# Scans and statistics in two tasks each, one table set for exp and log, a new steady order, and written-out lists for the last two and a half batches

## The reference, cut to what matters

```
delta = softplus(x @ Wd + bd);  B, C = x @ WB + bB, x @ WC + bC          # 16 states
for t in 1024 tokens:                                                    # for each of 16 states s
    h = clip(exp(min(delta*A, 2)) * h + clip(delta*B, -2, 2) * x, -100, 100)
    y = sum_s h * C + x * D_param
expert = argmax(softmax(y @ Wr + br)), weight = its probability          # 4 experts
moe = weight * (silu(y @ up_w[expert] + up_b) @ down_w[expert] + down_b)
x1 = layernorm(x + layernorm(y + moe) * ln_w + ln_b)
out = layernorm(x1 + (silu(x1 @ wg) * (x1 @ wu)) @ wd)                   # 384 hidden
```

## Time and profile before

| | |
|---|---|
| median of 3 runs | 922.79 us (919.44 to 923.1) |
| span of the profiled execution | 920.4 us (its own time is not listed beside it) |
| granted TensorE clock, mean | 0.837 |
| PE busy | 640.0 us (70%) |
| DVE busy | 715.4 us (78%) |
| ACT busy | 537.6 us (58%) |
| POOL busy | 566.2 us (62%) |
| chain that ended last | PE 30%, DVE 26%, issue 15%, ACT 15%, DMA 7% |
| L1209 + L1218, multiplies and scans | 166.7 + 163.8 + 155.4 us of DVE |

### The profile page before, as it was taken

How to read it: one execution, slowest core, us unless ns; L and a number is a source line. 1 busy time by engine, 2 the same in 40 slices (tenths; PEclk the granted TensorE clock), 3 DMA queues, 4 the chain that set the end, 5 groups by cost and what they waited for, 6 DMA issues and landing times.

```text
span 920.4 us, 14199 instructions
## 1 busy us (share of the span) xinstructions
PE 640.0 (70%) x4263; PEld 511.3 (56%) x4322; DVE 715.4 (78%) x1458; ACT 537.6 (58%) x988; POOL 566.2 (62%) x452
## 2 busy tenths in 40 slices
PE   3466658783799658973899379865896399638755
PEld 1234436672587437862778258743885277517624
DVE  3699897689988998799979998899879986432152
ACT  5373273664785749583876478565955276226422
POOL 1366548657964887568766787488747873562151
PEclk9576676996799869995999689986998599859968
DMA  3333344775367536754576536862574457325400
GB/s 102 128 127 115 138 149 148 243 225 189 112 218 237 197 96 190 239 166 153 163 243 202 188 113 219 247 203 85 203 240 138 156 166 247 89 82 154 135 23 24
DMA packets 82087, 149.31 MB, mean 162 GB/s; under 512 B 9404, under 2 KB 51144, under 8 KB 81992
## 3 DMA queue, kind: packets, MB, share of 16 engines
q1 hardware_dynamic: 69192, 135.13, 45.2%
q0 software_dynamic: 4096, 8.40, 2.8%
q10 hardware_dynamic: 8704, 4.72, 1.9%
HBM read 132.80 MB, written 15.40 MB: 161 GB/s over the span
## 4 chain that ended last, share of the span: by engine, by line
PE 30%; DVE 26%; issue 15%; ACT 15%; DMA 7%; POOL 4%; SPq 1%; another core or an unknown queue 0%; ACTq 0%; DVEq 0%; POOLq 0%
DVE state L1218 12%; DMA weights<-in_w_pack 5%; PE psY L561 4%; PE psU L691 4%; DVE psB L1209 4%; PE psD L585 4%; ACT hid L846 4%; PE psT L705 3%; ACT decay L807 3%; PE psU L732 2%; PE psU L734 2%; DVE bst L1152 2%; PE psB L555 2%; ACT L846 2%; PE psU L619 1%
## 5 line engine op out<-in xcount | busy, mean ns | idle before, releaser
L1245 POOL TENSOR_TENSOR prod<-state,c_wide 128x1024 f32<-128x1024 f32 x128 | 308.4, 2415 | 149.1 <-DVE state L1218 127.3
L1209 DVE TENSOR_TENSOR psB<-dx,psB 128x512 f32<-128x512 f32 x256 | 166.7, 689 | 31.6 <-PE psB L555 13.7
L1218 DVE TENSOR_TENSOR_SCAN state<-decay,state,psB 128x512 f32<-128x512 f32 x128 | 163.8, 1280 | 14.0
L555 PE MATMUL psB<-parts,sel 128*128 128x512 bf16 x198 | 89.5, 466 | 122.4 <-DVE state L1218 121.1
L1218 DVE TENSOR_TENSOR_SCAN state<-decay,psB 128x512 f32<-128x512 f32 x128 | 155.4, 1214 | 3.2 <-ACT decay L807 3.2
L561 PE MATMUL psY<-ident,prod 128*128 128x128 f32 x1024 | 155.0, 305 | 1.1 <-DVE state L1218 0.5
L807 ACT ACTIVATE decay<-delta,a_sb 128x1024 f32<-128x1024 f32 x128 | 142.0, 1141 | 15.7 <-DVE state L1218 7.4
L561 PEld LDWEIGHTS psY<-ident,prod 128*128 128x128 f32 x1024 | 137.5, 159 | 12.3 <-issue 7.9
L555 PEld LDWEIGHTS psB<-parts,sel 128*128 128x128 bf16 x256 | 25.8, 103 | 174.2 <-DVE state L1218 168.1
L846 ACT ACTIVATE hid<-psU,weights 128x128 f32<-128x128 f32 x352 | 99.7, 371 | 39.2 <-PE psU L691 33.7
L691 PE MATMUL psU<-yT_sorted,weights 128*128 128x128 f32 x704 | 96.1, 282 | 19.4 <-DMA weights<-in_w_pack 8.3
(11 more groups left out here) (165 smaller groups left out, 1080.4 us busy)
## 6 DMA issues: line engine op xcount, KB each, us to landing
c_wide<-c_rows SPq DMA_DIRECT2D x128, 512.0 KB, 5.2
weights<-in_w_pack SPq DMA_DIRECT2D x88, 514.0 KB, 4.2
xT_sb<-in_xT SPq DMA_DIRECT2D x8, 512.0 KB, 5.0
y_sorted<-rows_in SPq DMA_DIRECT2D x16, 256.0 KB, 3.1
xt<-in_x SPq DMA_DIRECT2D x8, 512.0 KB, 4.4
rows_out<-result SPq DMA_DIRECT2D x16, 256.0 KB, 4.3
out<-x ACTq DMA_DIRECT2D x16, 256.0 KB, 2.5
y_sorted<-rows_in SPq DMA_DIRECT2D x8, 192.0 KB, 4.5
```

The lines of the kernel that those rows point to most:

```text
L555: pe.matmul(tokens(psB, c, h), sel[:, s, :], parts[:, c.n % 2, h * HALF:h * HALF + c.hw], start=True, stop=True).then_inc(b_ready, 1)
L1209: v.tensor_tensor(tokens(psB, c, h), dx[:, n % 2, h * HALF:h * HALF + c.hw], tokens(psB, c, h), ALU.mult).then_inc(inp_ready, 1)
L1218: v.tensor_tensor_scan(state[:, g % NSTATE, t0:t0 + c.hw], decay[:, g % NDECAY, t0:t0 + c.hw], tokens(psB, c, h), before, ALU.mult, ALU.ad ...
L1245: g_.tensor_tensor(prod[:, g % NPROD, w], state[:, g % NSTATE, w], c_wide[:, g % NC, w], ALU.mult).then_inc(prod_ready, 1)
```

## The change

It adds no computation and takes none away.

- ScalarE names the table set for Exp and Ln (`natural_log_exp_and_others`) at its start and again before `softplus`, `decay` and `router_exp` whenever a silu or a gate came in between.
- `scan` keeps the two multiplies and the scan of the first half; the scan of the second half is a task of its own, `scan_rest`, with its own conditional. `stats` keeps bn_stats; bn_aggr is a task `aggr`.
- All five steady lists are new (their chunk numbers are counted from another start, so that (-2, ...) on VectorE or TensorE may be the same chunk that was (0, ...) before).
- The last lists are new and long: 230, 142, 136, 90 and 64 tasks for PE, ACT, DVE, POOL and SP. They begin in the scans of the last batch but one (its scan 11 on VectorE).

The diff, cut to its core:

```diff
+EXP_LN = "natural_log_exp_and_others"
 DVE_ORDER = [
-    (0, "scan", 8), (-2, "ff_mul", 0, 0), (-2, "ff_mul", 0, 1), (1, "b_max"), (0, "scan", 9), (-2, "ff_mul", 0, 2),
-    (0, "scan", 10), (1, "bc_low"), (-2, "affine", 1), (-2, "stats", 1, 1), (0, "scan", 11), (1, "bound", 0),
-    (-2, "stats", 0, 2), (0, "scan", 12), (0, "scan", 13), (1, "dx"), (1, "bound", 1), (1, "over"),
-    (-2, "ff_mul", 1, 0), (-2, "ff_mul", 1, 1), (-1, "router_pick"), (-2, "ff_mul", 1, 2), (0, "scan", 14),
-    (1, "flag"), (-2, "stats", 1, 2), (0, "scan", 15), (1, "scan", 0), (1, "scan", 1), (1, "scan", 2),
-    (0, "router_shift"), (1, "scan", 3), (0, "slots"), (-1, "combine", 0), (1, "scan", 4), (-1, "stats", 0, 0),
-    (1, "scan", 5), (-1, "centre", 0), (1, "scan", 6), (-1, "affine", 0), (-1, "stats", 0, 1), (1, "scan", 7),
-    (-1, "combine", 1), (-1, "stats", 1, 0), (-1, "centre", 1), (2, "delta"),
+    (-4, "aggr", 1, 0), (-2, "scan", 9), (-4, "ff_mul", 0, 2), (-4, "centre", 1), (-2, "scan_rest", 9),
+    (-2, "scan", 10), (-2, "scan_rest", 10), (-1, "bc_low"), (-1, "dx"), (-4, "affine", 1), (-4, "stats", 1, 1),
+    (-4, "aggr", 1, 1), (-2, "scan", 11), (-1, "bound", 0), (-4, "stats", 0, 2), (-4, "aggr", 0, 2),
+    (-2, "scan_rest", 11), (-2, "scan", 12), (-2, "scan_rest", 12), (-2, "scan", 13), (-2, "scan_rest", 13),
+    (-3, "router_pick"), (-1, "bound", 1), (-1, "over"), (-4, "ff_mul", 1, 0), (-4, "ff_mul", 1, 1), (-2, "scan", 14),
+    (-4, "ff_mul", 1, 2), (-2, "scan_rest", 14), (-1, "flag"), (-4, "stats", 1, 2), (-4, "aggr", 1, 2),
+    (-2, "scan", 15), (-2, "scan_rest", 15), (-1, "scan", 0), (-1, "scan_rest", 0), (-1, "scan", 1),
+    (-1, "scan_rest", 1), (-1, "scan", 2), (-1, "scan_rest", 2), (-2, "router_shift"), (-1, "scan", 3), (-2, "slots"),
+    (-3, "combine", 0), (-3, "stats", 0, 0), (-1, "scan_rest", 3), (-1, "scan", 4), (-3, "aggr", 0, 0),
+    (-1, "scan_rest", 4), (-1, "scan", 5), (-3, "centre", 0), (-3, "affine", 0), (-1, "scan_rest", 5),
+    (-3, "stats", 0, 1), (-3, "aggr", 0, 1), (-1, "scan", 6), (-1, "scan_rest", 6), (-1, "scan", 7), (0, "b_max"),
+    (0, "delta"), (-1, "scan_rest", 7), (-3, "combine", 1), (-1, "scan", 8), (-3, "stats", 1, 0),
+    (-1, "scan_rest", 8), (-3, "ff_mul", 0, 0), (-3, "ff_mul", 0, 1),
 ]
 POOL_ORDER = [
-    ...
-    (0, "prod", 2), (-1, "scatter", 0), (0, "prod", 3), (-1, "scatter", 1), (0, "prod", 4), (-2, "x_shift", 1),
-    (-2, "gather", 5), (-2, "gather", 6), (-2, "rstd", 0, 0), (-1, "scatter", 2), (-2, "gather", 7),
-    (-1, "scatter", 3), (-2, "rstd", 0, 1), (-1, "scatter", 4), (0, "prod", 5), (-1, "scatter", 5),
-    (-1, "scatter", 6), (-1, "scatter", 7), (-2, "rstd", 1, 0), (0, "prod", 6), (0, "prod", 7), (1, "bc_rest"),
+    ...
+    (-6, "rstd", 1, 2), (-4, "prod", 14), (-4, "prod", 15), (-3, "prod", 0), (-5, "gather", 0), (-5, "gather", 1),
+    (-5, "gather", 2), (-5, "gather", 3), (-3, "prod", 1), (-5, "gather", 4), (-3, "prod", 2), (-5, "gather", 5),
+    (-4, "scatter", 0), (-4, "scatter", 1), (-3, "prod", 3), (-5, "rstd", 0, 0), (-4, "scatter", 2),
+    (-4, "scatter", 3), (-4, "scatter", 4), (-5, "gather", 6), (-3, "prod", 4), (-5, "rstd", 0, 1), (-3, "prod", 5),
+    (-5, "gather", 7), (-4, "scatter", 5), (-4, "scatter", 6), (-4, "scatter", 7), (-3, "prod", 6), (-3, "prod", 7),
 ...
 PE_ORDER = [
-    (-2, "ff_up", 1, 1), (-1, "down", 6), (-1, "up", 7), (-2, "ff_up", 1, 2), (0, "spread", 14, 0),
-    (1, "b_spread", 1), (-2, "ff_up", 1, 3), (-2, "ff_up", 1, 4), (0, "spread", 14, 1), (-1, "down", 7),
+    (-1, "spread", 11, 0), (-1, "spread", 11, 1), (-2, "down", 2), (-2, "sort_turn", 2), (-2, "up", 3),
+    (0, "b_spread", 0), (-1, "add", 8), (-3, "ff_down", 0), (-3, "ff_part", 0, 0), (-3, "ff_part", 0, 1),
+    ...
+    (-1, "spread", 14, 0), (-3, "ff_up", 1, 0), (-3, "ff_up", 1, 1), (-2, "down", 6), (-2, "up", 7),
+    (0, "b_spread", 1), (-3, "ff_up", 1, 2), (-3, "ff_down", 1),
 ACT_ORDER = [
+    (-5, "norm", 1, 1), (-3, "decay", 15), (-4, "result", 3), (-4, "silu", 4), (-5, "norm", 0, 2), (-4, "result", 4),
+    (-4, "silu", 5), (-5, "x_high", 1), (-4, "silu", 6), (-5, "x_low", 1), (-4, "result", 5), (-5, "gate", 1, 0),
+    (-5, "gate", 1, 1), (-4, "result", 6), (-4, "silu", 7), (-5, "gate", 1, 2), (-2, "decay", 0), (-4, "result", 7),
+    (-4, "silu", 8), (-4, "silu", 9), (-4, "result", 8), (-5, "norm", 1, 2), (-4, "silu", 10), (-4, "result", 9),
+    (-4, "result", 10), (-2, "decay", 1), (-3, "y_copy"), (-2, "decay", 2), (-3, "yT_copy"), (-2, "decay", 3),
+    ...
 DVE_LAST = [
+    (-1, "dx"), (-2, "scan", 11), (-3, "router_pick"), (-4, "affine", 1), (-2, "scan_rest", 11), (-2, "scan", 12),
+    (-2, "scan_rest", 12), (-2, "scan", 13), (-4, "stats", 1, 1), (-2, "scan_rest", 13), (-2, "scan", 14),
+    (-1, "bound", 0), (-2, "scan_rest", 14), (-2, "scan", 15), (-2, "scan_rest", 15), (-1, "scan", 0),
+    (-1, "scan_rest", 0), (-1, "scan", 1), (-4, "stats", 0, 2), (-1, "scan_rest", 1), (-1, "scan", 2),
+    (-4, "aggr", 0, 2), (-1, "scan_rest", 2), (-1, "scan", 3), (-1, "scan_rest", 3), (-1, "scan", 4),
+    (-4, "aggr", 1, 1), (-1, "scan_rest", 4), (-1, "scan", 5), (-1, "scan_rest", 5), (-2, "router_shift"),
+    (-1, "scan", 6), (-2, "slots"), (-1, "scan_rest", 6), (-1, "scan", 7), (-1, "scan_rest", 7), (-1, "scan", 8),
+    (-1, "scan_rest", 8), (-1, "scan", 9), (-1, "scan_rest", 9), (-1, "bound", 1), (-1, "scan", 10),
+    (-1, "scan_rest", 10), (-1, "scan", 11), (-1, "scan_rest", 11), (-1, "scan", 12), (-4, "ff_mul", 1, 0),
+    (-4, "ff_mul", 1, 1), (-1, "over"), (-1, "scan_rest", 12), (-1, "scan", 13), (-1, "flag"), (-3, "combine", 0),
+    (-1, "scan_rest", 13), (-4, "ff_mul", 1, 2), (-3, "stats", 0, 0), (-4, "stats", 1, 2), (-1, "scan", 14),
+    (-4, "aggr", 1, 2), (-3, "aggr", 0, 0), (-1, "scan_rest", 14), (-1, "scan", 15), (-1, "scan_rest", 15),
+    ...
 PE_LAST = [
-    (-1, "warm"), (-1, "x_turn", 0), (-1, "x_rest", 0), (-1, "ff_up", 0, 0), (-1, "ff_up", 0, 1), (-1, "ff_up", 0, 2),
+    ...
+    (-1, "spread", 14, 1), (-1, "add", 11), (-1, "spread", 15, 0), (-1, "add", 12), (-1, "spread", 15, 1),
+    (-2, "sort_turn", 0), (-1, "add", 13), (-2, "up", 0), (-1, "add", 14), (-2, "up", 1), (-1, "add", 15),
+    (-1, "yT_turn"), (-2, "down", 0), (-2, "sort_turn", 1), (-2, "up", 2), (-2, "sort_turn", 2), (-1, "logits"),
+    (-3, "x_turn", 0), (-2, "down", 1), (-3, "x_rest", 0), (-1, "rank"), (-2, "up", 3), (-3, "ff_up", 0, 0),
+    ...
+    (-2, "down", 9), (-3, "x_turn", 1), (-2, "down", 10), (-3, "x_rest", 1), (-1, "sort_turn", 0),
+    (-3, "ff_up", 1, 0), (-1, "sort_turn", 1), (-1, "up", 0), (-1, "sort_turn", 2), (-1, "up", 1), (-1, "down", 0),
+    ...
+    (-1, "ff_part", 1, 1), (-1, "ff_part", 1, 2), (-1, "warm"),
 @@ ScalarE
+            table = ["exp"]
+            nc.scalar.preload_act_table_set(EXP_LN)
+            def exp_table():
+                if table[0] != "exp":
+                    nc.scalar.preload_act_table_set(EXP_LN)
+                    table[0] = "exp"
                 if name == "softplus":
+                    exp_table()
                 if name == "decay":
                     (s,) = args
+                    exp_table()
                 if name == "router_exp":
+                    exp_table()
                     act.wait_ge(filled[u], fills(u, c, ("up", k)))
+                    table[0] = "silu"
@@ VectorE
-                    ins.then_inc(stats_local, 1)
-                    dve.wait_ge(stats_local, 1)
-                    dve.sem_clear(stats_local)
+                    ins.then_inc(sampled[h], 1)
+                if name == "aggr":
+                    h, k = args
+                    dve.wait_ge(sampled[h], 3 * c.with_half[h] + k + 1)
                     for j in range(c.hj):
                         ins = v.bn_aggr(mv[:, h, j, :], bst[:, h, j, :])
-                        for h in range(c.halves):
-                            ...
+                        dve.wait_ge(inp_ready, spreads + 1)
+                        before = carry[:, s:s + 1] if c.follows else 0.0
+                        v.tensor_tensor_scan(state[:, g % NSTATE, 0:c.hw], decay[:, g % NDECAY, 0:c.hw],
+                                             tokens(psB, c, 0), before, ALU.mult, ALU.add
+                                             ).then_inc(first_scanned if c.halves == 2 else state_ready, 1)
                     dve.nop()
+                if name == "scan_rest":
+                    (s,) = args
+                    g = S * n + s
+                    with dve.If(clips[0] > 0):
+                        dve.nop()
+                    with dve.Else():
+                        dve.wait_ge(inp_ready, S * c.halves0 + s * c.halves + 2)
+                        dve.wait_ge(first_scanned, c.twos0 + s + 1)
+                        v.tensor_tensor_scan(state[:, g % NSTATE, HALF:c.w], decay[:, g % NDECAY, HALF:c.w],
+                                             tokens(psB, c, 1), state[:, g % NSTATE, HALF - 1:HALF], ALU.mult, ALU.add
```

(27 more changed lines are left out.)

187 lines of the change are left out of this document (121 added, 66 removed), and 11 rows, old and new, of tables (SP_LAST, SP_ORDER).

## The result

The changed kernel takes 934.75 us (median of 4 runs, 933.13 to 934.81), the kernel before beside it 922.94 (4 runs, 919.44 to 923.52): a ratio of 1.0131, 95% interval 1.011 to 1.0152, so 1.3% slower. The prediction was 872 us, faster with a chance of 0.87. The profiled execution has a span of 933.0 us against 920.4; its mean granted clock is nearly the same, 0.841 against 0.837.

The account below looks back on a forecast made before the run. It took a loop from router through scatters, experts and bound check to set the 99.4 us period, VectorE's load a little below. Last scan at 744 plus 125 after it plus 2.4 gave 871.5, say 872 us, range 855 to 888.

Parts of the forecast that it names:

- the new steady order: Steady period of all engines: shorter ways on GpSimd, TensorE and VectorE, -4.2 us a period, ends -11 and +6.
- the wait before the second bound check: VectorE waiting for TensorE to spread the maxima, 4.24 us before; a sign said still about 3 us.
- A misread row: Scan 11 of batch 6, read at 664.17, was predicted to start at 642 after the start and steady savings.
- Last lists until the last scan: From scan 11 of batch 6: VectorE's list 96 us plus 6 for waits, last scan ending at 744 (738 to 765).
- Last lists after it: After the last scan: two expert blocks 75 us, then 19.6 and 30.7; sum 125 us, ends 117 and 143.
- the forecast 0.85: Sign: TensorE above 0.85 busy in the first 75 us after the last scan.
- Table loads: ScalarE's function table loads: 58 as before, none between exp and log; only 1.28 us saved, at the start.
- Start: Kernel start: one table load of 1.28 us gone and dx moved into a wait, 1.13 us; together -2.4 us.
- The conditional at nothing: VectorE's 128 more tasks from splitting scans, each with a conditional, taken as 0; ends +13 and a little, and -14.
- GpSimd's way from the first product to the last scatter: In the steady period: 41.35 us shortened to about 38 as the first shift and slots wait leave it, -2.9.
- The slower one: Rival: expert blocks wait for late weights, lengthening the loop; periods 8.4 us longer, 935 us; chance 0.08.

Follow-up runs that it names:

- the best version: Kernel after with tasks moved away from GpSimd's products (eight moves, then gather 7 ahead of product 4, combine 1 ahead of b_max and delta): 870.91 us, ratio 0.9435.
- the four tasks moved: Kernel after with combine 1, centre 1 and affine 1 earlier on VectorE and gather 5 ahead of product 2 on GpSimd: 883.43 us, ratio 0.9573.

## Why the prediction was wrong, step by step

**The step that failed: the new steady order, "I take -4.2 a period".** It moved tasks at the durations that they had in the old order. Measured periods are 107.9, 109.4, 106.0, 107.5 and 104.8 us instead of 95, in the mean 7.7 longer than before, where the step's own ends were 11 shorter and 6 longer. The parts that the step counted did come: VectorE's time without work fell by 3.6 us, and the wait before the second bound check is 3.55 us (at 502.21) where 3 was forecast. What it left out is that six places of the new order stand beside GpSimd's elementwise instructions, and that these lengthen them. Up to scan 11 of batch 6 they add up to 73 us held, from the durations in the trace less those of the same instruction alone (combine 1 five times 7.1, chosen five times 2.85, affine 1 four times 2.1, centre 1 five times 0.87, over 5.7, rs 5.1), where before it was 12 (combine 1 9.9, rs 1, over 0.8): 61 us more.

**A misread row.** The multiply at 664.17 is that of scan 12; scan 11 of batch 6 starts at 655.99 before (first row below). With it the step's own working gives 655.99 - 22.2 = 633.8. The kernel after starts that scan at 693.53, 59.7 later, which the 61 us account for; the best version starts it at 633.54. The kernel before, then the kernel after with its last scan:

```profile
655.99 0.70 DVE L1209 TENSOR_TENSOR psB<-dx,psB 128x512 f32<-128x512 f32 x1
...
693.53 1.28 DVE L1329 TENSOR_TENSOR psB<-dx,psB 128x512 f32<-128x512 f32 x2
...
791.38 1.28 DVE L1348 TENSOR_TENSOR_SCAN state<-decay,state,psB 128x512 f32<-128x512 f32 x1
```

**Last lists until the last scan: 102, measured 99.1** (693.53 to 792.66). About right, with 2 of those us held (combine 0 of batch 5 at 776.39: 3.10 instead of 1.14).

**Last lists after it: 125, measured 140.3**, inside the step's upper end of 143. The first window has TensorE at 63.31 of 75 us, 0.84, just under the forecast 0.85; but the last expert result comes 83.5 us after the scan (876.12), not 75, and from there to the turn of the last batch's first half it is 28.4 us, not 19.6 (PE in order of time, with its waits):

```profile
868.56 0.63 PE L821 MATMUL psD<-ident,attn 128*128 128x128 f32 x4 [0.59 <-ACT x L985]
...
887.24 1.09 PE L821 MATMUL psD<-ident,attn 128*128 128x128 f32 x4 [4.98 <-ACT x L985]
...
904.55 1.09 PE L821 MATMUL psD<-ident,attn 128*128 128x128 f32 x4 [4.90 <-ACT x L985]
```

These are the halves of batch 6 and the first of batch 7, 17 to 19 us each: a half is a chain through four engines, and I had counted only TensorE's work in it. That is read from the trace and was not tried by an experiment; the best version still has 137.8 us there.

**The rest.** Table loads: 58 (28, 22, 7 and 1), none between exp and log: right. Start: the first bound check at 24.67 instead of 25.81, and the second half of the first scan at 35.29 instead of 36.51: 1.2 of the 2.4; but the traces of the other versions with the new steady lists, which start alike, have that second half at 34.92 to 36.29, and the splits in the old order have it at 35.15, so one trace can't tell how much of it is the change. The conditional at nothing: right, a bare scan takes 3.69 us (405.37 to 409.06) as 3.70 before, and the splits and the table set alone are some 5 us faster than before, not slower. GpSimd's way from the first product to the last scatter: 41.5 us (412.92 to 454.41) instead of 38; with the four tasks moved it is 38.8 (390.74 to 429.50), so the held VectorE had lengthened this too.

**The rivals.** The slower one named 935 us, and 934.75 came, but its mechanism (the weights) is not it: TensorE's wait for them is 3.8 us in 6 cases, where it was 8.3 in 15; the number agrees by accident. The chance of 0.87 for faster rested on a sum in which no term could grow where two engines are both busy.

That 870.91 lies by the predicted 872 is luck: errors of the sum cancel in it. The misread row is 8 us too late, the stretch to the last scan 6 us too long (96 in the best version for 102), the end 13 to 15 us too short, and the best version has more moves than the change.
